# A down projection whose moving operand holds both halves of the weights

## The chip, the cores and the metric

The kernel runs on one core of one Trainium2 chip. The metric is the time on the device in microseconds. A profile comes from one more execution of the same program; its times are counted from its first instruction. Matmuls run on TensorE, and five instruction streams (TensorE, VectorE, ScalarE, GpSimd and SyncE) are written out by hand and joined by semaphores only.

## What is computed

A layer of gated cross attention and then a mixture of experts, over 16 x 256 = 4096 tokens of width 256, in float32. The change lies in the second half:

```python
logits = xf @ w_router
scores = softmax(logits); expert_weights, expert_indices = top_k(scores, 2)
h = silu(einsum('td,edh->teh', xf, w1)) * einsum('td,edh->teh', xf, w3)
y = einsum('teh,ehd->ted', h, w2)
moe_out = einsum('te,ted->td', cw, y)            # cw: the two chosen weights of a token
shared = silu(xf @ ws1) * (xf @ ws3) @ ws2
out = shared / 3 + moe_out * 2 / 3
x = x + tanh(g_ffn[0]) * out
```

There are 8 experts and one shared expert, each with 512 hidden units.

## The kernel before

**Numbers in two halves.** Each float32 operand of a projection is split into a high half (what the fast matmul format holds) and a low half (the rest), and a product is the sum of three: high x high, low x high, high x low. `three` (L580) issues these three matmuls for each chunk k of 128 contraction rows. The weights of an expert lie in `w_h[p]` and `w_l[p]`, three sets p: two change between the routed experts, the third (`SHARED`) holds the shared expert.

**Tiles.** After the attention stage (to about 345 us), 50 tiles of 256 tokens follow one another on TensorE: 6 early shared tiles, 34 routed tiles (tokens gathered by expert, four or five tiles an expert), 10 late shared tiles (batches 6 to 15). Each has 24 matmuls for `w1` (`up1`), 24 for `w3` (`up3`) and 24 for `w2` (`down`), all with 256 moving columns. TensorE's order for tile g (function `tile`) is `up1(g)`, `up3(g)`, `down(g-1)`. The last tile is taken apart and ends the kernel.

**Who does what in a tile g.** ScalarE: `silu(g)` of `up1`'s banks, the high half of the next tile's tokens (`xg_h`), a copy of the result of `down(g-1)` out of bank 5, the high half of the gated values (`gT_h`). VectorE: for routed tiles a transposition (`turn_rows`, L1490), the low half of the next tokens (`xg_l`), `gated(g)`, which multiplies `sg` with `up3`'s banks into `gg` (L1502), and `g_low(g)`, the low half `gT_l` (L1292). `up1(g)` waits for `xl_ok` (`xg_l`), `up3(g)` for `g_ok` of the tile before, and `down(g)` for `gl_ok` (`gT_l`) and `y_ok` (the result bank is free again).

**Results of routed tiles.** ScalarE's `y_before` (L1159) waits for the landing of the scatter before (`y_st`) and copies the bank to `y_s`; GpSimd's `scatter_y` (L1835) then sends its rows to `y_d` by row numbers that SyncE has fetched after the same landing. Between scatters GpSimd cuts the weights of the expert after next (`cut`, L1699 and L1703) in three parts, two before the first scatter of an expert and one behind it.

**Results of late shared tiles.** VectorE adds them from the bank into `x2a` (`add_late`, L1613), then mixes two finished batches with the routed results (`mix`, L1621 and L1626, each two operations, and a wait on its own result between) and, from batch 11 on, adds routed results of the last two batches (`add_pair`, L1636). SyncE stores each mixed batch; `mix` waits for the store of two batches before.

## Time and profile before

| | |
|---|---|
| Median of 3 runs | 798.59 us (797.7 to 800.58) |
| Profiled execution | 794.88 us, of which its span is 793.0 us |
| TensorE matmul | 765.8 us busy, 97% of the span |
| Weight loads (beside the matmuls) | 686.7 us, 87% |
| VectorE | 532.5 us, 67% |
| ScalarE | 423.5 us, 53% |
| GpSimd | 427.4 us, 54% |
| Granted TensorE clock, mean | 0.996 of full speed |

A busy share is a mean over stages. The stretches differ: attention until about 345 us, early shared tiles until about 420, routed tiles until about 710, late shared tiles until the end.

### The profile page before, as it was taken

What the parts mean: (1) busy time and instruction counts of PE and PEld (TensorE: products, weight loads), DVE (VectorE), ACT (ScalarE), POOL (GpSimd) and SP (SyncE); (2) the same over time, 40 slices, a digit from 0 to 9 for tenths busy, and PEclk for the clock granted to TensorE, in tenths of its full rate; (3) what the DMA queues carried; (4) which work ended last, traced back from release to release, by engine and by line L of the source; (5) the groups of instructions that cost most, each with busy time, mean ns of one, the idle gap of its engine ahead of it and who ended that gap; (6) DMA issues with size and microseconds to landing.
All of it is one profiled execution on the core that took longest, in us unless ns stands there. A gap on an engine that the chain in (4) does not pass through costs nothing.

```text
span 793.0 us, 19410 instructions
## 1 busy us (share of the span) xinstructions
PE 765.8 (97%) x6965; PEld 686.7 (87%) x6966; DVE 532.5 (67%) x1108; ACT 423.5 (53%) x717; POOL 427.4 (54%) x498
## 2 busy tenths in 40 slices
PE   5789999999999998999999999999999999999998
PEld 5666777777777776779999999999999999999998
DVE  6766788999888888856764544454344454456897
ACT  5767877777777777663344333333333333333332
POOL 5633447776666655376572659475846493235000
PEclk9989999999999999999999999999999999999999
DMA  6864557776666654253453646454533323218522
GB/s 210 270 201 162 177 189 238 241 241 217 212 217 215 212 179 143 95 201 134 133 153 97 171 140 186 116 141 114 159 89 106 97 53 80 54 60 340 217 84 81
DMA packets 130689, 127.36 MB, mean 161 GB/s; under 512 B 55232, under 2 KB 113088, under 8 KB 130624
## 3 DMA queue, kind: packets, MB, share of 16 engines
q1 hardware_dynamic: 117008, 82.44, 34.7%
q0 software_dynamic: 13616, 44.08, 15.8%
q8 instruction: 37, 0.61, 0.3%
q14 instruction: 28, 0.23, 0.1%
HBM read 75.32 MB, written 50.91 MB: 159 GB/s over the span
## 4 chain that ended last, share of the span: by engine, by line
PE 70%; POOL 8%; DMA 7%; DVE 5%; issue 5%; ACT 3%; POOLq 1%; SPq 0%; ACTq 0%; DVEq 0%
PE bank L586 8%; PE bank L587 7%; PE bank L588 7%; PE bank L676 7%; PE bank_ss L645 6%; PE bank_ss L586 4%; PE bank_ss L588 4%; PE bank_sm L586 4%; PE bank_ss L587 4%; POOL w_l L1703 4%; PE bank_sm L587 4%; PE bank_sm L588 4%; PE bank_sm L660 4%; DMA y_d<-y_s,y_rows 3%; PE bank L683 3%
## 5 line engine op out<-in xcount | busy, mean ns | idle before, releaser
L1315 DVE TENSOR_REDUCE row_max<-bank_sm 128x4 f32<-128x1024 f32 x124 | 151.6, 1222 | 40.8 <-PE bank_sm L660 40.3
L1000 ACT ACTIVATE probs_T<-bank_ss 128x1024 f32<-128x1024 f32 x123 | 126.5, 1028 | 19.1 <-PE bank_ss L645 18.9
L1292 DVE TENSOR_TENSOR gT_l<-gg,gT_h 128x1024 fp32r<-128x1024 f32 x49 | 69.3, 1415 | 100.2 <-ACT gT_h L1149 100.1
L586 PE MATMUL bank_sm<-xg_h,w_h 128*128 128x256 f32 x400 | 113.4, 283 | 0.5 <-DVE xg_l L1292 0.5
L586 PE MATMUL bank_ss<-xg_h,w_h 128*128 128x256 f32 x400 | 113.3, 283 | 0.4 <-DVE gg L1502 0.4
L587 PE MATMUL bank_sm<-xg_h,w_l 128*128 128x256 f32 x400 | 112.9, 282 | 0.0
L588 PE MATMUL bank_ss<-xg_l,w_h 128*128 128x256 f32 x400 | 112.9, 282 | 0.0
L588 PE MATMUL bank_sm<-xg_l,w_h 128*128 128x256 f32 x400 | 112.9, 282 | 0.0
L587 PE MATMUL bank_ss<-xg_h,w_l 128*128 128x256 f32 x400 | 112.9, 282 | 0.0
L586 PE MATMUL bank<-w_h,gT_h 128*128 128x256 f32 x392 | 111.1, 284 | 1.6 <-DVE gT_l L1292 1.6
L587 PE MATMUL bank<-w_h,gT_l 128*128 128x256 f32 x392 | 110.9, 283 | 0.0
L588 PE MATMUL bank<-w_l,gT_h 128*128 128x256 f32 x392 | 110.7, 282 | 0.0
L1753 POOL TENSOR_TENSOR qk_s<-qk_s 128x512 fp32r<-128x512 f32 x32 | 41.2, 1288 | 92.7 <-ACT qk_s L1052 92.6
L1835 POOL DMA_INDIRECT y_d<-y_s,y_rows x68 | 70.8, 1041 | 17.0 <-issue 15.8
L1143 ACT ACTIVATE sg<-bank_sm 128x512 f32<-128x512 f32 x98 | 53.2, 596 | 47.9 <-PE bank_sm L588 47.9
L1052 ACT ACTIVATE qk_s<-bank,bqk_s 128x256 f32<-128x256 f32 (+1 forms) x128 | 53.5, 480 | 47.1 <-PE bank L588 47.1
L586 PEld LDWEIGHTS bank_sm<-xg_h,w_h 128*128 128x128 f32 x400 | 76.4, 191 | 1.3 <-DVE xg_l L1292 0.7
L586 PEld LDWEIGHTS bank_ss<-xg_h,w_h 128*128 128x128 f32 x400 | 76.3, 191 | 0.7 <-DVE gg L1502 0.7
L586 PEld LDWEIGHTS bank<-w_h,gT_h 128*128 128x128 f32 x392 | 74.8, 191 | 2.2 <-DVE gT_l L1292 2.2
L587 PEld LDWEIGHTS bank_ss<-xg_h,w_l 128*128 128x128 f32 x400 | 76.4, 191 | 0.0
L587 PEld LDWEIGHTS bank_sm<-xg_h,w_l 128*128 128x128 f32 x400 | 76.4, 191 | 0.0
L588 PEld LDWEIGHTS bank_ss<-xg_l,w_h 128*128 128x128 f32 x400 | 76.4, 191 | 0.0
(210 smaller groups left out, 1956.0 us busy)
## 6 DMA issues: line engine op xcount, KB each, us to landing
qk_d<-qk_s SPq DMA_DIRECT2D x64, 256.0 KB, 2.7
w_raw<-wall POOLq DMA_DIRECT2D x27, 512.0 KB, 3.9
k<-qk_d SPq DMA_DIRECT2D x48, 256.0 KB, 3.9
q<-qk_d SPq DMA_DIRECT2D x48, 256.0 KB, 4.5
xq<-xs_d SPq DMA_DIRECT2D x140, 64.0 KB
y_pairs<-y_d POOLq DMA_DIRECT2D x16, 512.0 KB, 9.8
xs_d<-zero_rows SPq DMA_DIRECT2D x8, 514.0 KB, 4.6
x<-x SPq DMA_DIRECT2D x16, 256.0 KB, 4.3
```

Source lines behind the costliest of these rows:

```text
L586: pe.matmul(out, ah, bh, start=first and k == 0, stop=False)
L587: pe.matmul(out, al, bh, start=False, stop=False)
L588: r = pe.matmul(out, ah, bl, start=False, stop=last and k == n - 1)
L645: r = pe.matmul(exp_bank(V.b, pv)[:, par * 512 + half * L:par * 512 + (half + 1) * L], k4[V.slot][own, pv, half * P:(half + 1) * P], q4[V. ...
L676: r = pe.matmul(OT[g % 2][PVW * i:PVW * (i + 1), :], v_s[V.v_slot][:, kc, h, :], pT[:, h % 8, kc * L:(kc + 1) * L], start=kc == 0, stop=kc ...
L1000: act.activation(pT[:, 2 * (pv % 4):2 * (pv % 4) + 2, :].rearrange("p h t -> p (h t)"), exp_bank(V.b, pv)[:, :], ACT.Exp, scale=D ** -0.5) ...
L1052: r = act.activation(dst.bitcast(F32) if half else dst, bnk[:, oc * L:(oc + 1) * L], ACT.Identity, bias=bqk_s[:, 2 * side + oc:2 * side + ...
L1143: r = act.activation(sg[:, 2 * n:2 * n + 2, :].rearrange("p f t -> p (f t)"), psH1[n][:, :], ACT.Silu)
L1292: return v.tensor_tensor(dst, ps, high.bitcast(F32), ALU.subtract)
L1315: v.tensor_reduce(mx[B.slot][:, :, :].rearrange("p t (q r) -> p r t q", r=2)[:, :, :, p], max_bank(B.b, p)[:, :].rearrange("p (r t k) -> p ...
L1753: po.tensor_tensor(rest, rest.bitcast(F32), high.bitcast(F32), ALU.subtract).then_inc(done, 1)
L1835: po.indirect_dma_start(out=yd, out_offset=bass.IndirectOffsetOnAxis(ap=to[:, t:t + 1].bitcast(U32), axis=0), in_=y_s[:, t, :], in_offset= ...
```

## The change

The high and low halves of a set of weights become one tensor, `w_hl[p]`, so that one matmul can stream the high and the low half of the same 256 columns as one moving operand of 512. Result banks 5 and 6 become one tensor `Y2`. In the wide form of `down`, each chunk has one matmul of `gT_h` with both halves (512 columns) and one of `gT_l` with the high half (256 columns) instead of three of 256. The result of a tile then lies in two parts, `y_parts[0]` and `y_parts[1]`, whose sum is wanted. Wide are the projections of the 34 routed tiles and of the late shared tiles but the last; the six early ones stay as they were.

For routed tiles ScalarE copies the second part to `y_b` (`y_rest`), and VectorE adds it to the first part into `y_s` (`y_sum`, between `gated` and `g_low`), after waiting for the landing of the scatter before. For late shared tiles `add_late`, and the same step for batch 14, is two operations with a wait on the first's result between.

```diff
@@ -156,8 +156,8 @@
         wraw = sb(keep, "w_raw", [P, WSZ])
-        w_h0 = sb(keep, "w_h0", [P, WSZ], F32R)
-        w_l0 = sb(keep, "w_l0", [P, WSZ], F32R)
+        w0 = sb(keep, "w0", [P, 2, WSZ], F32R)
+        w_h0, w_l0 = w0[:, 0, :], w0[:, 1, :]
         tab = sb(keep, "table", [1, TW], I32)
...
@@ -233,17 +233,14 @@
             with ExitStack() as w:
-                w_h, w_l = [], []
-                for i in range(2):
-                    w_h.append(sb(w, f"w_h{i + 1}", [P, WSZ], F32R))
-                    w_l.append(sb(w, f"w_l{i + 1}", [P, WSZ], F32R))
-                w_h.append(w_h0)
-                w_l.append(w_l0)
+                w_hl = [sb(w, f"w_hl{i + 1}", [P, 2, WSZ], F32R) for i in range(2)] + [w0]
+                w_h, w_l = [u[:, 0, :] for u in w_hl], [u[:, 1, :] for u in w_hl]
             yg = sb(m, "y_pairs", [P, NB, TS, 2, E])
             x2a = sb(m, "x2_all", [P, NB, TS * E])
             xq = sb(m, "xq", [P, TR // QD, FQ])
             y_s = sb(m, "y_s", [P, TS, E])
+            y_b = sb(m, "y_rest", [P, TS, E])
             go = sb(m, "go", [P, 2])
...
@@ -264,7 +261,11 @@
         bank = [SS[:, 0:512], SS[:, 512:1024], SM[:, 0:512], SM[:, 512:1024]]
-        bank += [keep.enter_context(nc.psum_tensor(f"bank{i}", [P, 512], F32)) for i in range(4, 8)]
+        bank.append(keep.enter_context(nc.psum_tensor("bank4", [P, 512], F32))[:, :])
+        Y2 = keep.enter_context(nc.psum_tensor("bank56", [P, 1024], F32))
+        bank += [Y2[:, 0:512], Y2[:, 512:1024]]
+        bank.append(keep.enter_context(nc.psum_tensor("bank7", [P, 512], F32))[:, :])
+        y_parts = [Y2[:, :].rearrange("p (t s d) -> p t s d", t=TS, s=2)[:, :, n, :] for n in range(2)]
...
@@ -612,10 +613,24 @@
-            def down(g, p):
+            def down(g, p, wide=False):
                 pe.wait_ge(gl_ok, g + 1)
                 pe.wait_ge(y_ok, g + 1)
+                if wide:
+                    for t in range(TS):
+                        def high(k):
+                            return pe.matmul(Y2[:, t * 2 * E:(t + 1) * 2 * E].rearrange("p (s d) -> p s d", s=2), gT_h[:, k, t * P:(t + 1) * P],
+                                             w_hl[p][:, :, W2O + k * E:W2O + (k + 1) * E], start=k == 0, stop=k == FC - 1)
+
+                        for k in range(FC):
+                            if k < FC - 1:
+                                high(k)
+                            pe.matmul(Y2[:, t * 2 * E:t * 2 * E + E], gT_l[:, k, t * P:(t + 1) * P],
+                                      w_h[p][:, W2O + k * E:W2O + (k + 1) * E], start=False, stop=False, skip_group_check=True)
+                        r = high(FC - 1)
+                    r.then_inc(w2_ps, 1)
+                    return
                 for t in range(TS):
...
@@ -912,11 +927,11 @@
-            def tile(g, p, before):
+            def tile(g, p, before, wide=True):
                 up1(g, p)
                 up3(g, p)
-                down(g - 1, before)
+                down(g - 1, before, wide)
...
@@ -926,7 +941,7 @@
                 pe.wait_ge(w_ok, k * WP + 2 * WP)
-                tile(tb, p, before)
+                tile(tb, p, before, before != SHARED)
                 te = ends if isinstance(ends, list) else [value(T_E, k + i, EARLY + 2, EARLY + NT) for i in range(ends)]
...
@@ -955,7 +970,7 @@
                 r.then_inc(last_up, 1)
-            down(end + (NB - 2 - EARLY), SHARED)
+            down(end + (NB - 2 - EARLY), SHARED, True)
             for n in range(2):
...
@@ -1152,11 +1167,10 @@
-            def y_before(g, sent):
+            def y_rest(g):
                 act.wait_ge(w2_ps, g)
-                moved(act, y_st, sent * 32)
-                act.activation(y_s[:, :, :].rearrange("p t d -> p (t d)"), psY[:, :], ACT.Copy).then_inc(y_ok, 1)
+                act.activation(y_b[:, :, :], y_parts[1], ACT.Copy).then_inc(yb_ok, 1)
...
@@ -1203,22 +1217,22 @@
             x_high_routed(EARLY + 2)
-            y_before(EARLY + 1, 0)
+            y_rest(EARLY + 1)
             g_high(EARLY + 1)
             with act.Fori(1, last2) as u:
                 silu(u + (EARLY + 1))
                 x_high_routed(u + (EARLY + 2))
-                y_before(u + (EARLY + 1), u)
+                y_rest(u + (EARLY + 1))
                 g_high(u + (EARLY + 1))
             silu(last)
             x_high_shared(EARLY, end)
-            y_before(last, last2)
+            y_rest(last)
             g_high(last)
             for j in range(EARLY, NB - 1):
                 silu(end + (j - EARLY))
                 x_high_shared(j + 1, end + (j + 1 - EARLY))
                 if j == EARLY:
-                    y_before(end, last2 + 1)
+                    y_rest(end)
                 g_high(end + (j - EARLY))
...
@@ -1507,6 +1521,12 @@
+            def y_sum(copied, sent):
+
+                v.wait_ge(yb_ok, copied)
+                moved(v, y_st, sent)
+                v.tensor_tensor(y_s[:, :, :], y_parts[0], y_b[:, :, :], ALU.add).then_inc(y_ok, 1)
+
             iterations(v, one)
...
@@ -1597,11 +1617,18 @@
                 score_weights(b)
-            with v.Fori(EARLY + 1, last) as g:
-                turn_rows(g + 1)
-                x_low_routed(g + 1)
-                gated(g)
-                g_low(g)
+            last2 = v.value_load(tab[0:1, T_L2:T_L2 + 1], min_val=2 * NX - 2, max_val=NT - 2)
+            turn_rows(EARLY + 2)
+            x_low_routed(EARLY + 2)
+            gated(EARLY + 1)
+            y_sum(1, 0)
+            g_low(EARLY + 1)
+            with v.Fori(1, last2) as u:
+                turn_rows(u + (EARLY + 2))
+                x_low_routed(u + (EARLY + 2))
+                gated(u + (EARLY + 1))
+                y_sum(u + 1, u * 32)
+                g_low(u + (EARLY + 1))
...
@@ -1610,7 +1637,9 @@
                 v.wait_ge(w2_ps, end + (j + 1 - EARLY))
-                v.scalar_tensor_tensor(x2a[:, j, :], psY[:, :], gsc[:, 0:1], x2a[:, j, :], ALU.mult, ALU.add).then_inc(y_ok, 1)
+                x2j = x2a[:, j, :].rearrange("p (t d) -> p t d", t=TS)
+                link(v.scalar_tensor_tensor(x2j, y_parts[0], gsc[:, 0:1], x2j, ALU.mult, ALU.add))
+                v.scalar_tensor_tensor(x2j, y_parts[1], gsc[:, 0:1], x2j, ALU.mult, ALU.add).then_inc(y_ok, 1)
...
@@ -1649,6 +1679,8 @@
                         add_pair(*PAIR_AT[j])
+                    if j == EARLY:
+                        y_sum(last2 + 2, (last2 + 1) * 32)
                     g_low(end + (j - EARLY))
...
@@ -1673,7 +1705,9 @@
             v.wait_ge(o_st[b % 2], (b // 2) * 16)
-            v.scalar_tensor_tensor(o_o[b % 2][:, :, :].rearrange("p t d -> p (t d)"), psY[:, :], gsc[:, 0:1], x2a[:, b, :], ALU.mult, ALU.add).then_inc(mix_ok, 1)
+            x2b = x2a[:, b, :].rearrange("p (t d) -> p t d", t=TS)
+            link(v.scalar_tensor_tensor(x2b, y_parts[0], gsc[:, 0:1], x2b, ALU.mult, ALU.add))
+            v.scalar_tensor_tensor(o_o[b % 2][:, :, :], y_parts[1], gsc[:, 0:1], x2b, ALU.mult, ALU.add).then_inc(mix_ok, 1)
             b = NB - 1
```

TensorE, a down projection in the loop of late shared tiles, before (the names give result, stationary and moving operand, and the moving columns stand last):

```order
L586 MATMUL bank<-w_h,gT_h 128x256
L587 MATMUL bank<-w_h,gT_l 128x256
L588 MATMUL bank<-w_l,gT_h 128x256
L586 MATMUL bank<-w_h,gT_h 128x256
L587 MATMUL bank<-w_h,gT_l 128x256
L588 MATMUL bank<-w_l,gT_h 128x256
```

And the same place in the changed kernel:

```order
L623 MATMUL bank<-w,gT_h 128x512
L629 MATMUL bank<-w,gT_l 128x256
L623 MATMUL bank<-w,gT_h 128x512
L629 MATMUL bank<-w,gT_l 128x256
L623 MATMUL bank<-w,gT_h 128x512
L629 MATMUL bank<-w,gT_l 128x256 x2
L623 MATMUL bank<-w,gT_h 128x512 x2
```

Of 24 matmuls and weight loads a tile 16 are left, with the same 6144 columns; the last of four chunks has its short matmul first.

VectorE, the loop over routed tiles, before:

```order
L1490 STREAM_TRANSPOSE bank<-xq 128x512
L1494 REGISTER_ALU
L1292 TENSOR_TENSOR xg_l<-bank,xg_h 128x512
L1502 TENSOR_TENSOR gg<-sg,bank_ss 128x512 x2
L1292 TENSOR_TENSOR gT_l<-gg,gT_h 128x1024
```

And in the changed kernel:

```order
L1504 STREAM_TRANSPOSE bank<-xq 128x512
L1508 REGISTER_ALU
L1306 TENSOR_TENSOR xg_l<-bank,xg_h 128x512
L116 REGISTER_ALU
L1516 TENSOR_TENSOR gg<-sg,bank_ss 128x512 x2
L1526 REGISTER_ALU
L116 REGISTER_ALU
L1528 TENSOR_TENSOR y_s<-bank,y_rest 128x512
L1306 TENSOR_TENSOR gT_l<-gg,gT_h 128x1024
```

The add stands ahead of `gT_l`, for which TensorE's down projection waits.

VectorE, a late shared tile with mixes and a pair, before:

```order
L1292 TENSOR_TENSOR xg_l<-xsT,xg_h 128x512
L1502 TENSOR_TENSOR gg<-sg,bank_ss 128x512 x2
L1636 SCALAR_TENSOR_TENSOR x_all<-y_pairs,router_wts,x_all 128x256 x2
L1292 TENSOR_TENSOR gT_l<-gg,gT_h 128x1024
L1613 SCALAR_TENSOR_TENSOR x_all<-bank,gate_scaled,x_all 128x512
L1621 SCALAR_TENSOR_TENSOR y_pairs<-y_pairs,router_wts,x_all 128x256 x2
L1626 SCALAR_TENSOR_TENSOR oo<-y_pairs,router_wts 128x256 x2
```

And in the changed kernel:

```order
L1306 TENSOR_TENSOR xg_l<-xsT,xg_h 128x512
L1516 TENSOR_TENSOR gg<-sg,bank_ss 128x512 x2
L1665 SCALAR_TENSOR_TENSOR x_all<-y_pairs,router_wts,x_all 128x256 x2
L1306 TENSOR_TENSOR gT_l<-gg,gT_h 128x1024
L1641 SCALAR_TENSOR_TENSOR x_all<-bank,gate_scaled,x_all 128x512
L1642 SCALAR_TENSOR_TENSOR x_all<-bank,gate_scaled,x_all 128x512
L1650 SCALAR_TENSOR_TENSOR y_pairs<-y_pairs,router_wts,x_all 128x256 x2
L1655 SCALAR_TENSOR_TENSOR oo<-y_pairs,router_wts 128x256 x2
```

One operation more stands ahead of the mixes, and behind them the next tile's `xg_l`.

## Rows read from the trace of the kernel before

**Rows 1.** Table of stretches: start:end, length, busy us and (instructions) per engine, clock, DMA.

```profile
600.00:715.00 115.00, 115.00 (x962) 115.00 (x962) 53.79 (x70) 42.99 (x67) 59.97 (x63) 1.00 0.28 76
715.00:770.00 55.00, 55.00 (x464) 55.00 (x463) 43.30 (x79) 17.74 (x26) 11.70 (x17) 1.00 0.62 228
...
sum 793.00, PE 765.83 PEld 686.67 DVE 532.47 ACT 423.55 POOL 427.37; mean PE 127.64 PEld 114.45 DVE 88.75 ACT 70.59 POOL 71.23
```

**Rows 2.** Page, costliest groups: count, busy us, mean ns, idle before.

```profile
L586 PE MATMUL bank<-w_h,gT_h 128*128 128x256 f32 x392 | 111.1, 284 | 1.6 <-DVE gT_l L1292 1.6
```

**Rows 3.** Warm-up by line L628, ns min/median/max; timelines: start, us, then what.

```profile
L628 PEld LDWEIGHTS bank_ss<-wt_h x14: 187/188/189, 18.4 to 25.9; 128*128 128x128 f32 x14
L628 PE MATMUL bank_ss<-wt_h x14: 388/390/397, 18.5 to 26.2; 128*128 128x512 f32 x14
...
18.53 1.76 PE L628 MATMUL bank_ss<-wt_h 128*128 128x512 f32 x7
...
331.74 0.97 PEld L745 LDWEIGHTS bank<-wr_s,xn2T 128*128 128x128 f32 x8 [0.18 <-ACT xn2T L1013]
```

**Rows 4.** TensorE's waits, 440 to 600: us, times, longest; then the chain of waits.

```profile
PE bank L586 <- DVE gT_l L1292: 1.6, 3, 0.7
...
575.07 1.67 DVE gT_l L1292
576.78 0.39 PE bank L586
```

**Rows 5.** Timeline of ScalarE: y_s copies, in brackets idle before and its releaser.

```profile
439.46 0.60 ACT L1159 ACTIVATE y_s<-bank 128x512 f32<-128x512 f32 x1 [2.30 <-PE bank L588]
...
573.49 0.60 ACT L1159 ACTIVATE y_s<-bank 128x512 f32<-128x512 f32 x1 [5.13 <-DMA y_d<-y_s,y_rows]
...
616.49 0.60 ACT L1159 ACTIVATE y_s<-bank 128x512 f32<-128x512 f32 x1 [4.04 <-DMA y_d<-y_s,y_rows]
```

**Rows 6.** Timeline of GpSimd and of VectorE while expert weights are cut.

```profile
445.08 2.55 POOL L1703 TENSOR_TENSOR w_l<-w_raw,w_h 128x512 fp32r<-128x512 f32 x2
...
449.65 3.53 POOL L1703 TENSOR_TENSOR w_l<-w_raw,w_h 128x512 fp32r<-128x512 f32 x2
...
446.44 1.27 DVE L1502 TENSOR_TENSOR gg<-sg,bank_ss 128x512 f32<-128x512 f32 x2
449.68 2.35 DVE L1292 TENSOR_TENSOR gT_l<-gg,gT_h 128x1024 fp32r<-128x1024 f32 x1 [1.97 <-ACT gT_h L1149]
```

**Rows 7.** Timeline of VectorE, late shared tiles.

```profile
759.13 0.69 DVE L1292 TENSOR_TENSOR xg_l<-xsT,xg_h 128x512 fp32r<-128x512 f32 x1
759.74 1.28 DVE L1502 TENSOR_TENSOR gg<-sg,bank_ss 128x512 f32<-128x512 f32 x2
...
762.14 1.23 DVE L1292 TENSOR_TENSOR gT_l<-gg,gT_h 128x1024 fp32r<-128x1024 f32 x1 [0.34 <-ACT gT_h L1149]
763.29 0.74 DVE L1613 SCALAR_TENSOR_TENSOR x_all<-bank,gate_scaled,x_all 128x512 f32<-128x512 f32 x1
763.95 0.87 DVE L1621 SCALAR_TENSOR_TENSOR y_pairs<-y_pairs,router_wts,x_all 128x256 f32<-128x256 f32 x2
764.86 0.88 DVE L1626 SCALAR_TENSOR_TENSOR oo<-y_pairs,router_wts 128x256 f32<-128x256 f32 x2
...
767.37 0.69 DVE L1292 TENSOR_TENSOR xg_l<-xsT,xg_h 128x512 fp32r<-128x512 f32 x1
...
770.68 1.23 DVE L1292 TENSOR_TENSOR gT_l<-gg,gT_h 128x1024 fp32r<-128x1024 f32 x1 [0.62 <-ACT gT_h L1149]
```

**Rows 8.** Timeline of VectorE, late shared tiles of batches 8 and 9.

```profile
724.50 0.69 DVE L1292 TENSOR_TENSOR xg_l<-xsT,xg_h 128x512 fp32r<-128x512 f32 x1 [3.38 <-ACT xg_h L1132]
...
741.65 0.88 DVE L1626 SCALAR_TENSOR_TENSOR oo<-y_pairs,router_wts 128x256 f32<-128x256 f32 x2 [0.73 <-DMA out<-oo]
```

**Rows 9.** Timeline of VectorE, the end.

```profile
788.44 0.74 DVE L1676 SCALAR_TENSOR_TENSOR oo<-bank,gate_scaled,x_all 128x512 f32<-128x512 f32 x1
789.67 0.48 DVE L1681 SCALAR_TENSOR_TENSOR oo<-bank,gate_scaled,x_all 128x256 f32<-128x256 f32 x1 [0.48 <-PE bank L588]
```

More of the change, by code:

```diff
@@ L304, in build @@
         gh_ok = sem("gh_ok"); gl_ok = sem("gl_ok"); w2_ps = sem("w2_ps"); last_up = sem("last_up"); last_sg = sem("last_sg"); last_g = sem("last_g"); last_gh = sem("last_gh"); last_gl = sem("last_gl"); last_w2 = sem("last_w2"); last_mix = sem("last_mix"); last_st = sem("last_st")
-        y_ok = sem("y_ok"); y_st = sem("y_st"); to_in = sem("to_in"); go_ok = sem("go_ok"); tok_ok = sem("tok_ok"); x2_in = sem("x2_in")
+        y_ok = sem("y_ok"); yb_ok = sem("yb_ok"); y_st = sem("y_st"); to_in = sem("to_in"); go_ok = sem("go_ok"); tok_ok = sem("tok_ok"); x2_in = sem("x2_in")
         yg_in = [sem(f"yg_in{i}") for i in range(NB)]
@@ L1641, in _ @@
             gated(last)
+            y_sum(last2 + 1, last2 * 32)
             g_low(last)
```

## The prediction

> **What bounds the kernel now.** I read the table of stretches first, then TensorE's own waits, then the chain of waits backwards from each of them. TensorE is busy for 765.8 of 793 us, and without a gap from 600 to 770, while VectorE has work for 43.3 of the 55 us from 715 to 770 [rows 1]. So a step that TensorE loses there is gained, as long as nobody else is nearly late. Two parties are nearly late, and the busy shares hide both.
>
> The first is GpSimd from 440 to 600. TensorE's only waits in the routed tiles are three for `gT_l`, the longest 0.7 us by that view, one each in three of the experts [rows 4]. The chain leads back from the one at 576.78 over `gT_l` [rows 4] and `gT_h` to the `y_s` copy at 573.49, which a scatter's landing released, and from there for 130 us over GpSimd and its transfers alone (cutting weights, scatter, landing, row numbers, scatter) to the copy at 439.46 [rows 5]. In that stretch GpSimd sets the pace by a hair.
>
> The second is VectorE in the late shared tiles. One tile there runs from 759.13 to 767.37, 8.24 us, and in it VectorE waits for nothing but 0.34 us for `gT_h`, which itself follows VectorE's own `gg` [rows 7]. TensorE needs 55.00/464 x 72 = 8.53 us a tile [rows 1]. This is a serial chain with a slack of 0.3 us a tile, not an engine with a fifth of its time free.
>
> **What the change removes.** A tile has 72 matmuls of 256 columns, 24 of them down, at 115.00/962 = 0.120 us each [rows 1]; a triple takes 0.36. The wide form issues one of 512 and one of 256. The only 512-column stream is the warm-up at 18.53: seven in 1.76 us, the last lasting 0.39, so (1.76 - 0.39)/6 = 0.229 us each [rows 3]. A triple becomes 0.229 + 0.120 = 0.349: 0.011 saved, 8 triples a tile, 0.09 us. There are 392 such triples in 49 down projections [rows 2], the last tile's aside; six early shared ones stay narrow, 43 go wide: 3.8 us in all. The ends: nothing (the two-piece moving operand costs what the load saved), and 0.035 a triple (0.28 a tile) if the loads are what sets 0.12 now; loads alone come every (0.97 - 0.19)/7 = 0.111 us [rows 3]. I take 0.011, since its row has both a full load and 512 columns in each step.
>
> The Trainium skill, "TensorE: Matmul & The Clock Gate", section "Back-to-back issue gap", gives 262 cycles for 256 columns and 518 for 512, so that merging two saves 6 cycles, 2.5 ns: 0.9 us over 344 triples where the rows say 3.8. The spacing of 120 ns here is 11 above that page's 109, so I hold to the rows.
>
> **What of that arrives, routed tiles.** ScalarE's copy goes to `y_b` and no longer waits for the scatter; VectorE does the waiting and adds, 0.64 us (as half of the `gg` pair, also one PSUM and one SBUF operand [rows 7]), between `gated` and `g_low`. Behind it on VectorE stand `g_low`, for which TensorE's next down projection waits, and the row turn.
> Where TensorE sets the pace the add runs beside ScalarE's `gT_h` of 1.05 and costs nothing. But `y_ok` comes 0.7 us later and GpSimd's scatter with it. So GpSimd's chain starts at 439.46 with three wide projections gained (-0.27) and 0.7 lost: 0.45 us later. At 573.49 its landing is thus at 573.94. From there before: copy, `gT_h`, `gT_l` (1.67), start at 576.78, 3.29 us [rows 4, 5]. After: add 0.6, `gT_l` 1.67, semaphores 0.05 to 0.1, 2.35 to 2.8, since `gT_h` is already done; I take 2.77, since the add may be stretched beside GpSimd's `w_l` as `gT_l` is in [rows 6]. The projection starts at 576.7 - 0.5 = 576.26: only **0.5 us** of the 1.5 us saved up to there is kept, and TensorE waits some 1.0 us more than before in sum. Five tiles later, at the landing of 616.49 [rows 5], the two are level again: 0.9. From there 11 routed projections bring 11 x 0.09 = 1.0. At 715 us TensorE is **2.0 us early** (ends: 0 and 5, the latter with 0.28 a tile over 16 tiles and 0.5 before).
>
> **What of that arrives, late shared tiles.** `add_late` becomes two operations with a wait on its own result between. One takes 0.74, 0.66 to the next start; where VectorE waits on its own result now, the next starts 0.04 after the end instead of 0.08 before [rows 7]. So each adds 0.74 + 0.04 = 0.78 us to VectorE. The first of the eight falls into 3.38 us of idle [rows 8]. The other seven stand in tiles with two mixes: 7 x 0.78 = 5.5 us on a chain with no idle. It absorbs the two waits for stored outputs (0.73 [rows 8] and one of 0.2) and the excess of the last two `gT_h` waits over 0.34 (0.62 [rows 7], so 0.3 each): 1.5 us. The end of the kernel hangs on this chain: the final up projections wait for `gated` of batch 14, and VectorE's last multiplications for the mixes before them. Behind them the doubled add at 788.44 ends at 789.9 rather than 789.2 and moves the next one, at 789.67 [rows 9], by 0.2, of which the last keeps 0.1. Sum: 5.5 - 1.5 + 0.1 = **4.1 us later**; TensorE's 9 wide projections here bring 0.2 (three before VectorE takes over), the rest is lost in new waits of about 0.5 us before each `up1`.
>
> **Sum.** 794.88 - 2.0 - 0.2 + 4.1 = 796.8 us for the profiled execution, +1.9. The median is 798.59 of runs from 797.7 to 800.58, above the profiled one by 3.7; I carry the difference over: **800.5 us**.
>
> **The rivals.**
> *GpSimd is slowed (slower).* `w_l` takes 2.55 us for two passes, but 3.53 where `gT_l` falls on it [rows 6]: 0.98 for one collision. If the new add, or a `gT_l` shifted onto a pass, costs that once in each expert from the third on, the landing at 576 comes 3 us later, at 616 4 us; TensorE enters the late tiles 2.1 us behind instead of 2.0 ahead, and the late loss stays: +6, 804.6. It decides from some 0.5 us per expert on. For it: there is no slack in GpSimd's chain. Against: the add has one operand in PSUM, like `gg`, and `gg` at 446.44 ran beside the 2.55 row [rows 6] without stretching it.
> *The late additions hide (faster, within 0.5%).* VectorE is idle for 11.7 us from 715 to 770, and 8 x 0.78 is 6.2 [rows 1]. Then 2.0 + 0.7 come through: 795.9. Against it is the serial order in [rows 7].
> *Loads set the spacing.* 0.28 a tile: 5.0 early at 715, then VectorE's chain paces the rest and takes 3.6 back: 797.2. The same page's section "LDWEIGHTS" has columns / 1.2, 107 ns for 128; by it the wide pair would cost 216 + 109 ns, this rival. The warm-up [rows 3] has 0.229 where that load is hidden, against it.
> *The wide form saves nothing.* 0.5 early at 715, 4.1 late: 802.2.
>
> **How the numbers follow.** A change of 0.5%, 4 us, is about what a measurement here can tell from none. Forecast 0.55; loads 0.12; hidden 0.10; no saving 0.08; GpSimd slowed 0.12; something else 0.03. Of the forecast's and the no-saving case's own spread (1.5 us in the sum, 1 us in a median of three) some 0.1 lies beyond 802.6. So faster 0.07, same 0.74, slower 0.19. The range takes in loads and hidden and half of the GpSimd case: 795.8 to 804.0.
>
> **What would show it.** Spacing in the profile after: 0.23 behind each 512-column matmul, 0.12 behind the 256 (0.35 a pair); 0.325 speaks for loads. A down projection of 2.79 instead of 2.88. Waits for `gT_l` near 497, 541 and 577, of 1 us or more. In the late tiles VectorE's pitch 9.0, with TensorE waiting some 0.5 before each `up1` from batch 11 on, and about 1.8 before the last. `w_l` passes no longer than before. I am wrong if the late pitch stays at 8.5 (hidden), or if TensorE is late already at 715 us (GpSimd).

## The result, and the profile after

The changed kernel takes 800.01 us (median of 20 runs, 795.82 to 803.58), the kernel before 797.26 us (20 runs, 794.65 to 802.27). The medians differ by 2.8 us. The ratio, which isn't quite the quotient of the medians, is 1.0036 with a 95% interval of 1.0020 to 1.0051 (1.6 to 4.1 us longer): a small loss, within the 0.5% that I called no change. The forecast was 800.5 us.

The profiled execution has a span of 797.0 us where the kernel before had 793.0. I split it at two points that both traces show: A, the first matmul of `up1` of the second routed tile (the last before any wide projection), and B, the first matmul of `up1` of batch 8, the third late tile. Between them lie 34 routed down projections and one late one. I call the last part, from B on, the end stage.

| | start to A | A to B | B to end | span |
|---|---|---|---|---|
| before | 413.27 | 304.61 | 75.12 | 793.0 |
| after | 415.20 | 301.56 | 80.24 | 797.0 |
| difference | +1.93 | -3.05 | +5.12 | +4.0 |

The first difference is not the change's: nothing in that part is computed otherwise, and over all profiles of this study A lies anywhere from 412.88 to 416.81, the earliest in a kernel with wide projections, the latest in one with narrow ones.

First the page's lines of busy time and of the costliest groups that answer to [rows 2], and the table of stretches that answers to [rows 1] (start:end, length, busy us and instructions of TensorE, its weight loads, VectorE, ScalarE and GpSimd, then clock and DMA).

```profile
PE 764.6 (96%) x6621; PEld 668.3 (84%) x6622; DVE 556.9 (70%) x1151; ACT 426.2 (53%) x717; POOL 430.3 (54%) x498
...
L623 PE MATMUL bank<-w_hl,gT_h 128*128 128x512 f32 x272 | 96.0, 396 | 1.6 <-DVE gT_l L1306 1.5
```

```profile
600.00:715.00 115.00, 115.00 (x865) 110.30 (x864) 63.40 (x84) 43.78 (x68) 63.54 (x63) 1.00 0.28 76
715.00:770.00 55.00, 53.13 (x394) 49.95 (x393) 44.84 (x80) 16.68 (x24) 11.79 (x17) 1.00 0.60 218
770.00:797.00 27.00, 21.54 (x156) 19.53 (x154) 22.14 (x41) 6.20 (x9) 0.00 (x0) 1.00 0.24 80
```

TensorE is still full from 600 to 715, and no longer from 715 on: it is without work for 1.9 of the 55 us there, and for 5.5 in the last stretch, what follows its last matmul among them. TensorE's own timeline shows both, a routed projection without a wait and two late tiles that begin with one.

```profile
448.39 0.39 PE L623 MATMUL bank<-w_hl,gT_h 128*128 128x512 f32 x1
448.62 0.28 PE L629 MATMUL bank<-w_hl,gT_l 128*128 128x256 f32 x1
448.74 0.40 PE L623 MATMUL bank<-w_hl,gT_h 128*128 128x512 f32 x1
...
752.11 0.40 PE L623 MATMUL bank<-w,gT_h 128*128 128x512 f32 x1
752.81 0.39 PE L587 MATMUL bank_sm<-xg_h,w 128*128 128x256 f32 x1 [0.30 <-DVE xg_l L1306]
...
781.14 0.36 PE L587 MATMUL bank_sm<-xg_h,w 128*128 128x256 f32 x1 [1.48 <-DVE gg L1516]
```

A pair takes 448.74 - 448.39 = 0.35 us, of which 0.23 behind the 512 columns. At 752.81 the next matmul would have been due at 752.11 + 0.23 = 752.34, so 0.47 are lost.

TensorE's waits, first from 440 to 600 [rows 4], then from 715 to the end (in all, times, longest):

```profile
PE bank L623 <- DVE gT_l L1306: 1.5, 1, 1.5
...
PE bank_sm L587 <- DVE xg_l L1306: 2.1, 4, 1.3
PE bank_sm L587 <- DVE gg L1516: 1.5, 1, 1.5
```

VectorE's timeline in the late tiles, which answers to [rows 7] and [rows 8] (in brackets idle before, and its releaser):

```profile
741.40 0.88 DVE L1655 SCALAR_TENSOR_TENSOR oo<-y_pairs,router_wts 128x256 f32<-128x256 f32 x2 [0.60 <-DMA out<-oo]
743.05 0.69 DVE L1306 TENSOR_TENSOR xg_l<-xsT,xg_h 128x512 fp32r<-128x512 f32 x1 [0.76 <-ACT xg_h L1147]
...
752.07 0.69 DVE L1306 TENSOR_TENSOR xg_l<-xsT,xg_h 128x512 fp32r<-128x512 f32 x1
...
755.08 1.22 DVE L1306 TENSOR_TENSOR gT_l<-gg,gT_h 128x1024 fp32r<-128x1024 f32 x1 [0.34 <-ACT gT_h L1164]
756.23 0.74 DVE L1641 SCALAR_TENSOR_TENSOR x_all<-bank,gate_scaled,x_all 128x512 f32<-128x512 f32 x1
757.00 0.75 DVE L1642 SCALAR_TENSOR_TENSOR x_all<-bank,gate_scaled,x_all 128x512 f32<-128x512 f32 x1
757.67 0.87 DVE L1650 SCALAR_TENSOR_TENSOR y_pairs<-y_pairs,router_wts,x_all 128x256 f32<-128x256 f32 x2
...
761.09 0.68 DVE L1306 TENSOR_TENSOR xg_l<-xsT,xg_h 128x512 fp32r<-128x512 f32 x1
```

From one `xg_l` to the next, the pitch of VectorE's chain, it is 761.09 - 752.07 = 9.02 us, where it was 8.24 [rows 7]. The second addition is the whole difference: it starts 0.77 behind the first, and the only idle time in the tile is the same 0.34 for `gT_h`. The end, which answers to [rows 9]:

```profile
792.10 0.74 DVE L1709 SCALAR_TENSOR_TENSOR x_all<-bank,gate_scaled,x_all 128x512 f32<-128x512 f32 x1
792.88 0.75 DVE L1710 SCALAR_TENSOR_TENSOR oo<-bank,gate_scaled,x_all 128x512 f32<-128x512 f32 x1
793.55 0.48 DVE L1715 SCALAR_TENSOR_TENSOR oo<-bank,gate_scaled,x_all 128x256 f32<-128x256 f32 x1
```

### The profile page after: what moved, and what is told of

The parts are those of the page before. It is cut to its first block, busy times and chain, and to the rows that moved or that the text cites. A ratio compares the mean times of both kernels' runs of the same rounds, so it can differ in the third digit from the quotient of the medians.

```text
span 797.0 us, 18828 instructions
## 1 busy us (share of the span) xinstructions
PE 764.6 (96%) x6621; PEld 668.3 (84%) x6622; DVE 556.9 (70%) x1151; ACT 426.2 (53%) x717; POOL 430.3 (54%) x498
## 4 chain that ended last, share of the span: by engine, by line
PE 63%; DVE 10%; POOL 8%; DMA 8%; issue 6%; ACT 3%; POOLq 1%; SPq 0%; DVEq 0%; ACTq 0%
PE bank L691 7%; PE bank_ss L660 6%; PE bank L587 5%; PE bank L623 5%; POOL w_hl L1737 4%; PE bank L588 4%; PE bank L589 4%; PE bank_sm L675 4%; PE bank_ss L587 3%; PE bank_ss L589 3%; PE bank_ss L588 3%; PE bank_sm L587 3%; PE bank_sm L588 3%; PE bank_sm L589 3%; DMA y_d<-y_s,y_rows 3%
## 5 line engine op out<-in xcount | busy, mean ns | idle before, releaser
L623 PE MATMUL bank<-w_hl,gT_h 128*128 128x512 f32 x272 | 96.0, 396 | 1.6 <-DVE gT_l L1306 1.5
L589 PE MATMUL bank_ss<-xg_l,w_hl 128*128 128x256 f32 x272 | 77.1, 284 | 0.0
L588 PE MATMUL bank_sm<-xg_h,w_hl 128*128 128x256 f32 x272 | 77.1, 283 | 0.0
L587 PE MATMUL bank_ss<-xg_h,w_hl 128*128 128x256 f32 x272 | 77.1, 283 | 0.0
L589 PE MATMUL bank_sm<-xg_l,w_hl 128*128 128x256 f32 x272 | 77.0, 283 | 0.0
L588 PE MATMUL bank_ss<-xg_h,w_hl 128*128 128x256 f32 x272 | 76.9, 283 | 0.0
L587 PE MATMUL bank_sm<-xg_h,w_hl 128*128 128x256 f32 x272 | 76.8, 282 | 0.0
L1737 POOL TENSOR_TENSOR w_hl<-w_raw,w_hl 128x512 fp32r<-128x512 f32 x48 | 71.8, 1515 | 2.0
L1776 POOL DMA_INDIRECT xs_d<-xn,slot_i x64 | 64.2, 1003 | 15.6 <-issue 14.3
L691 PE MATMUL bank<-probs_T,v 128*32 128x256 f32 x1024 | 69.4, 389 | 0.0
L660 PE MATMUL bank_ss<-q,k 64*128 64x256 f32 x492 | 63.0, 333 | 5.8 <-ACT probs_T L1015 5.4
L1516 DVE TENSOR_TENSOR gg<-sg,bank_ss 128x512 f32<-128x512 f32 x98 | 62.5, 680 | 5.8 <-PE bank_ss L589 5.8
```

Source lines behind the costliest of these rows:

```text
L587: pe.matmul(out, ah, bh, start=first and k == 0, stop=False)
L588: pe.matmul(out, al, bh, start=False, stop=False)
L589: r = pe.matmul(out, ah, bl, start=False, stop=last and k == n - 1)
L623: return pe.matmul(Y2[:, t * 2 * E:(t + 1) * 2 * E].rearrange("p (s d) -> p s d", s=2), gT_h[:, k, t * P:(t + 1) * P], w_hl[p][:, :, W2O + ...
L660: r = pe.matmul(exp_bank(V.b, pv)[:, par * 512 + half * L:par * 512 + (half + 1) * L], k4[V.slot][own, pv, half * P:(half + 1) * P], q4[V. ...
L691: r = pe.matmul(OT[g % 2][PVW * i:PVW * (i + 1), :], v_s[V.v_slot][:, kc, h, :], pT[:, h % 8, kc * L:(kc + 1) * L], start=kc == 0, stop=kc ...
```

## The experiments

All medians, intervals and parts in one table; each kernel ran beside the kernel before on the same chip. Differences in microseconds below are worked out from the ratio, which differs from the quotient of the two medians by up to about 0.1% (for "routed wide only" the medians are 2.6 us apart and the ratio gives 2.0). A to B and B to end are read from the one profiled execution, and so are TensorE's waits in the routed tiles (waits of 0.15 us and more); one execution differs there from the next, so a difference of a microsecond between two rows can be chance.

| kernel | median | before beside it | ratio [95%] | A to B | routed waits | B to end |
|---|---|---|---|---|---|---|
| before | | | | 304.61 | 1.6 | 75.12 |
| after | 800.01 | 797.26 | 1.0036 [1.0020, 1.0051] | 301.56 | 1.5 | 80.24 |
| routed wide only | 793.27 | 795.87 | 0.9975 [0.9954, 0.9995] | 301.87 | 1.5 | 76.14 |
| late wide only | 799.83 | 795.87 | 1.0051 [1.0034, 1.0068] | 304.58 | 1.7 | 78.89 |
| added operation only | 799.98 | 795.87 | 1.0050 [1.0033, 1.0068] | 305.10 | 2.2 | 78.87 |
| result path only | 795.24 | 795.87 | 0.9996 [0.9979, 1.0013] | 302.97 | 0.2 | 76.34 |
| GpSimd adds | 800.78 | 796.78 | 1.0055 [1.0038, 1.0071] | 303.42 | 3.0 | 81.71 |
| GpSimd adds, load first | 800.88 | 796.78 | 1.0049 [1.0031, 1.0068] | 304.94 | 3.6 | 81.38 |
| after, load first | 799.39 | 796.78 | 1.0032 [1.0017, 1.0046] | 304.06 | 3.5 | 79.42 |
| routed wide, load first | 794.01 | 796.78 | 0.9963 [0.9945, 0.9980] | 303.35 | 2.9 | 75.15 |
| the same, sum behind `gT_l` | 792.77 | 797.66 | 0.9933 [0.9908, 0.9957] | 299.90 | 0.2 | 75.54 |
| before, load first | 798.89 | 797.66 | 1.0004 [0.9979, 1.0029] | 306.01 | 2.8 | 75.18 |

### The two halves of the change apart

Routed tiles wide, the late ones and batch 14 as before with one addition (the main lines):

```diff
-                tile(g, SHARED, SHARED)
+                tile(g, SHARED, SHARED, False)
...
-                link(v.scalar_tensor_tensor(x2j, y_parts[0], gsc[:, 0:1], x2j, ALU.mult, ALU.add))
-                v.scalar_tensor_tensor(x2j, y_parts[1], gsc[:, 0:1], x2j, ALU.mult, ALU.add).then_inc(y_ok, 1)
+                v.scalar_tensor_tensor(x2a[:, j, :], psY[:, :], gsc[:, 0:1], x2a[:, j, :], ALU.mult, ALU.add).then_inc(y_ok, 1)
```

> Wide down projections for the 34 routed tiles only; the late shared tiles are narrow again with one add each. Theory (two separate terms, a gain in the routed tiles and a loss on VectorE's late chain): about 3 us faster than the kernel before (2 by the prediction's sum, 3.05 by the trace of the changed kernel), ratio 0.996 to 0.9975, down projection 2.80 us, late VectorE pitch 8.2 to 8.5 as before. Rival (the 1.9 us by which the changed kernel's trace is late already at 400 us comes from the merged weight tensors): it stays here, so only 1 us faster and the first wide projection again 1.9 us late. Rival (GpSimd's chain takes the routed gain): no change.

Late tiles wide, the routed ones as before (ScalarE's `y_before` straight to `y_s`; the main lines):

```diff
-                    tile(g, p, p)
+                    tile(g, p, p, False)
...
-                act.activation(y_b[:, :, :], y_parts[1], ACT.Copy).then_inc(yb_ok, 1)
+                moved(act, y_st, sent * 32)
+                act.activation(y_s[:, :, :].rearrange("p t d -> p (t d)"), psY[:, :], ACT.Copy).then_inc(y_ok, 1)
```

> Routed tiles narrow with ScalarE's copy as in the kernel before; only the late shared tiles are wide with the doubled add. Theory (VectorE's serial chain is the bound there): 4 to 5 us slower, ratio 1.005 to 1.0065, VectorE's pitch 9.0 us from batch 10 on, TensorE waits 0.3 to 0.7 before each of its first up projections from batch 11 and 1.5 to 1.9 before the last tile. Rival (the additions hide in VectorE's idle time): 0.7 us faster, no such waits.

The first is 2.0 us faster than before (0.4 to 3.7), the second 4.1 slower (2.7 to 5.4). Their sum, +2.1, agrees with the +2.8 of the whole within the intervals. So the change is a gain and a loss that nearly cancel, each in its own stage.

### The added operation by itself

The kernel before, with its narrow projections, and a second addition of zero times the bank behind the first, with the same wait between. Batch 14, not shown, has it too:

```diff
-                v.scalar_tensor_tensor(x2a[:, j, :], psY[:, :], gsc[:, 0:1], x2a[:, j, :], ALU.mult, ALU.add).then_inc(y_ok, 1)
+                link(v.scalar_tensor_tensor(x2a[:, j, :], psY[:, :], gsc[:, 0:1], x2a[:, j, :], ALU.mult, ALU.add))
+                v.scalar_tensor_tensor(x2a[:, j, :], psY[:, :], zero[:, 0:1], x2a[:, j, :], ALU.mult, ALU.add).then_inc(y_ok, 1)
```

> The kernel before, all projections narrow, with a second, linked add (times zero, from the same bank) behind each late add and behind that of batch 14: the added VectorE work alone, no wide matmul, no second bank. Theory: 4.1 us slower or up to 5, ratio 1.005 to 1.0065, pitch 9.0. Rival (the wide matmuls or the two-bank operand cost the time in the late tiles, not the operation): under 1 us slower.

It costs 4.0 us (2.6 to 5.4), as much as the wide late projections with their two additions. The end stage is 78.87 us long against 78.89 with the wide form: in the late tiles the wide form of TensorE brings and costs nothing that shows, and VectorE's operation is the whole loss. VectorE's timeline of this kernel has the pitch again, 771.20 - 762.19 = 9.01 us:

```profile
762.19 0.68 DVE L1292 TENSOR_TENSOR xg_l<-xsT,xg_h 128x512 fp32r<-128x512 f32 x1
...
766.34 0.74 DVE L1613 SCALAR_TENSOR_TENSOR x_all<-bank,gate_scaled,x_all 128x512 f32<-128x512 f32 x1
767.12 0.75 DVE L1614 SCALAR_TENSOR_TENSOR x_all<-bank,zero_rows,x_all 128x512 f32<-128x512 f32 x1
...
771.20 0.68 DVE L1292 TENSOR_TENSOR xg_l<-xsT,xg_h 128x512 fp32r<-128x512 f32 x1
```

### The path of the routed results by itself

The changed kernel with every projection narrow; the routed results still go over `y_b` on ScalarE and an operation on VectorE. The maximum of the bank and its own copy stands for the sum, so that the operation keeps its operands and nothing is left out:

```diff
-                v.tensor_tensor(y_s[:, :, :], y_parts[0], y_b[:, :, :], ALU.add).then_inc(y_ok, 1)
+                v.tensor_tensor(y_s[:, :, :].rearrange("p t d -> p (t d)"), psY[:, :], y_b[:, :, :].rearrange("p t d -> p (t d)"), ALU.max).then_inc(y_ok, 1)
```

> All projections narrow; only the way of the routed results is the changed one: ScalarE copies to y_b, VectorE waits for the scatter and forms y_s (here the larger of two equal values). Theory (the path is nearly neutral: y_ok 0.7 us later, 0.5 us back at the waits): within 1 us of before, w_l passes as long as before, waits for gT_l 0.5 us shorter each. Rival (GpSimd slowed): 2 us slower or more, with more passes of 3.5 us. If the path by itself gains, the routed gain of 3 us is partly not the matmuls': then 1 us faster.

The time does not move (-0.3 us, -1.7 to +1.0), but the trace does: TensorE waits 0.2 us for `gT_l` where it waited 1.6, and A to B is 1.6 us shorter than in the kernel before. That fits the prediction's view that it pays when `gT_h` no longer stands behind the landing. But it is one execution, and in the six kernels below that use this path with wide projections the waits are 1.5 to 3.6 us; how much of the routed gain is the path's and how much the matmuls' is not shown. The end stage gives 1.2 back: TensorE waits 1.1 us for tokens there, which leads to the next edit.

### The added operation on GpSimd

GpSimd is idle in the late tiles, so there the second part might cost nothing: ScalarE scales it into `y_b`, and GpSimd adds it. TensorE's next projection then waits for ScalarE's copy as well, and the projection of batch 14 is narrow again (both not shown).

```diff
+                    act.activation(y_b[:, :, :], y_parts[1], ACT.Identity, bias=zero[:, 0:1], scale=gsc[:, 0:1]).then_inc(yb_ok, 1)
...
-                link(v.scalar_tensor_tensor(x2j, y_parts[0], gsc[:, 0:1], x2j, ALU.mult, ALU.add))
-                v.scalar_tensor_tensor(x2j, y_parts[1], gsc[:, 0:1], x2j, ALU.mult, ALU.add).then_inc(y_ok, 1)
+                v.scalar_tensor_tensor(x2j, y_parts[0], gsc[:, 0:1], x2j, ALU.mult, ALU.add).then_inc(y_ok, 1)
...
+                po.tensor_tensor(x2j, x2j, y_b[:, :, :], ALU.add).then_inc(x2b_ok, 1)
```

> The changed kernel, except that in the late shared tiles VectorE keeps one addition: ScalarE copies the second result part, scaled by the gate, to y_rest, and GpSimd, which is idle there, adds it to the output sum; the last tile but one has the narrow projection. Theory (VectorE's serial chain paces the late tiles, and the added operation of 0.78 us is the whole loss): the late stage falls back from 80.2 us (first late tile to the end, changed kernel) to about 76 to 76.5, as where the late projections are narrow; time against the kernel before -1.5 to -2.5 us. Rival A (the wide form itself, or ScalarE's copy of 0.6 us behind the projection, holds the tiles): the late stage stays above 79, time +2 to +4. Rival B (GpSimd's additions of some 1.3 us slow VectorE where both run): pitch of the tiles with two mixes between 8.6 and 9.0 us, time 0 to +2.

My theory missed by some 6 us here: 4.4 us slower than before (3.0 to 5.7), an end stage of 81.71 us. VectorE's chain still sets the pace, and the time of the operation did not leave it. GpSimd's and VectorE's timelines:

```profile
757.97 1.40 POOL L1906 TENSOR_TENSOR x_all<-x_all,y_rest 128x512 f32<-128x512 f32 x1 [7.87 <-DVE x_all L1651]
```

```profile
757.08 0.74 DVE L1651 SCALAR_TENSOR_TENSOR x_all<-bank,gate_scaled,x_all 128x512 f32<-128x512 f32 x1
757.74 1.91 DVE L1660 SCALAR_TENSOR_TENSOR y_pairs<-y_pairs,router_wts,x_all 128x256 f32<-128x256 f32 x2
759.68 0.88 DVE L1665 SCALAR_TENSOR_TENSOR oo<-y_pairs,router_wts 128x256 f32<-128x256 f32 x2
760.48 0.88 DVE L1660 SCALAR_TENSOR_TENSOR y_pairs<-y_pairs,router_wts,x_all 128x256 f32<-128x256 f32 x2
```

While GpSimd adds from 757.97 to 759.37, VectorE's pair of mixes takes 1.91 us instead of the 0.88 of the same pair at 760.48: 1.03 us lost in place of the 0.77 that were taken away. All six such pairs from 738 us on take 1.91, each beside a GpSimd addition. The pitch is 9.27 us, which is 8.24 + 1.03. Rival B had the mechanism and too small a price.

### The load of the tokens

In the changed kernel TensorE waits 1.33 us before batch 11. VectorE's `xg_l` at 743.05 waited for ScalarE, and ScalarE for a load, by its timeline and SyncE's:

```profile
742.39 0.63 ACT L1147 ACTIVATE xg_h<-xsT 128x512 fp32r<-128x512 f32 x1 [4.47 <-DMA xsT<-xT_d]
```

```profile
731.03 2.10 SPq L563 DMA_DIRECT2D out<-oo  x2
733.29 0.38 SPq L465 DMA_DIRECT2D xsT<-xT_d  x1
```

SyncE issues it behind the two stores, and it lands 9.1 us later. Meanwhile the 16 `y_pairs` loads of GpSimd's queue are on the DMA engines: issued from 716.0 to 726.9, they take 4.9 to 15.3 us from issue to landing, and the last is in at 742.1. The next load of tokens, issued at 742.85, takes 2.7. The edit issues each such load one tile earlier, ahead of the stores (the one for batch 8, the loop's first instruction until now, stands ahead of the loop):

```diff
+            load_shared(EARLY + 2, total + (EARLY + 1))
             for j in range(EARLY + 2, NB):
-                load_shared(j, total + (j - 1))
+                if j + 1 < NB:
+                    load_shared(j + 1, total + j)
```

It was put on four kernels. On that with routed tiles wide and late ones narrow:

> Routed tiles wide, late tiles narrow with one addition on VectorE, and SyncE's load of a late batch's tokens ahead of the stores. Theory (as for the previous kernel): routed tiles wide alone gave -2.0 us (793.27 against 795.87) with TensorE waiting 0.7 us for tokens near 743 us; without that wait -2.7 to -3.3 us, the late stage 75.3 us instead of 76.1. Rival (the wait only moves): -2.0 us as before, the late stage 76.

On the changed kernel:

> The changed kernel with the load of a late batch's tokens ahead of the stores, and nothing else. Theory A (the late tiles are one serial chain on VectorE from batch 9 on, and a wait for tokens stretches it): -1.0 to -1.5 us against the changed kernel, so +1.3 to +1.8 against the kernel before; the late stage 79 us. Theory B (the chain on VectorE is late at 743 us by its own work, the tokens are not what it waits for): +2.8 as the changed kernel, the late stage 80.

On the one with GpSimd's addition:

> The previous kernel with one more edit: SyncE issues the load of a late batch's tokens ahead of the stores of the two mixed batches, one tile earlier. Theory (the tokens of batch 11, landing at about 742.3 us whether TensorE is early or not, give back about 1 us of what the routed tiles won): the wait of TensorE for xg_l near 743 us (1.5 us in the changed kernel) goes, and the time is 0.7 to 1.5 us below that of the previous kernel. Rival (VectorE's chain or its wait for the store of two batches before is late there anyway, or the load is as late behind the y_pairs loads): the wait moves to another name and the time is the same within 0.3 us.

And on the kernel before:

> The kernel before, with SyncE's load of a late batch's tokens ahead of the stores of the mixed batches. Theory (the load's landing at about 742 us is a limit only for a TensorE that comes early, since the kernel before has no wait of TensorE there): within 0.5 us of the kernel before, the late stage 75 us as there. Rival (the order of loads and stores is worth about 1 us by itself): -1 us.

With the routed tiles wide it is 2.9 us faster than the kernel before (1.6 to 4.4), TensorE's wait for tokens is gone and the end stage is 75.15 us instead of 76.14, as the theory had it. The kernel before gains nothing (+0.3 us, -1.7 to +2.3; end stage 75.18): the landing limits only a TensorE that comes early. On the changed kernel the wait falls from 1.3 to 0.4 us and the end stage by 0.8, between the two theories; its time, 1.0032, can't be told from 1.0036. With GpSimd's addition the wait falls from 1.5 to 1.2 only and the time is the same, which is the rival. The times of the two kernels with routed tiles wide, 0.9963 and 0.9975, can't be told apart either, so the 1.0 us rests on the profiles.

### The sum behind `gT_l`

The waits in the routed tiles remain, 1.5 to 3.6 us in the six kernels that are wide there. In VectorE's timeline of the changed kernel one looks like this:

```profile
497.54 0.69 DVE L1528 TENSOR_TENSOR y_s<-bank,y_rest 128x512 f32<-128x512 f32 x1 [5.32 <-DMA y_d<-y_s,y_rows]
498.15 1.46 DVE L1306 TENSOR_TENSOR gT_l<-gg,gT_h 128x1024 fp32r<-128x1024 f32 x1
```

The low half stands behind the landing and the addition. The last edit to the best kernel so far turns them round in the routed tiles:

```diff
-                y_sum(u + 1, u * 32)
                 g_low(u + (EARLY + 1))
+                y_sum(u + 1, u * 32)
```

> Routed tiles wide, late tiles narrow, token loads ahead of the stores, as in the kernel that gave 794.0 us against 796.8; and in the routed tiles VectorE's addition into y_s stands behind gT_l instead of ahead of it. Where the scatter's landing is late (498 and 577 us, TensorE idle 1.5 and 1.4 us), TensorE then waits for 0.7 us behind the landing instead of 2.1. Theory A (what counts is the place of gT_l behind the wait): both waits go, 1.4 to 2.9 us faster than that kernel, about -4.5 against the kernel before. Theory B (GpSimd's chain is full from about 440 us on, so the landing is as late as the first addition of the chain starts later, about 1.3 us): the waits stay within 0.5 us of what they were, under the name of the addition's semaphore, and the time is the same within 0.5 us: about -2.8 against the kernel before.

Theory A held, and theory B fell: 5.3 us faster than the kernel before (3.4 to 7.3), the best of all. TensorE has one wait of 0.2 us left in the routed tiles. B was right that the first addition, and with it GpSimd's chain, starts later, but wrong that the chain has no slack. GpSimd's timeline, first with the sum ahead of `gT_l`, then behind:

```profile
440.99 0.19 POOL L1865 TENSOR_TENSOR go<-go 128x1 f32<-128x1 f32 x1 [4.80 <-DVE y_s L1530]
441.33 1.82 POOL L1867 DMA_INDIRECT y_d<-y_s,y_rows  x1 [0.15 <-issue]
...
450.95 3.41 POOL L1735 TENSOR_TENSOR w_hl<-w_raw,w_hl 128x512 fp32r<-128x512 f32 x2
...
463.54 0.22 POOL L1865 TENSOR_TENSOR go<-go 128x1 f32<-128x1 f32 x1
```

```profile
443.74 0.19 POOL L1865 TENSOR_TENSOR go<-go 128x1 f32<-128x1 f32 x1 [5.95 <-DVE y_s L1530]
444.08 0.99 POOL L1867 DMA_INDIRECT y_d<-y_s,y_rows  x1
...
452.93 2.55 POOL L1735 TENSOR_TENSOR w_hl<-w_raw,w_hl 128x512 fp32r<-128x512 f32 x2
...
464.53 0.22 POOL L1865 TENSOR_TENSOR go<-go 128x1 f32<-128x1 f32 x1
```

It starts 2.75 us later, of which 0.76 lie before A (414.36 here, 413.60 there), and is 0.99 later two scatters on: the first scatter's issue no longer runs beside `gT_l` (0.99 instead of 1.82), and one pass of the cut does not either (2.55 instead of 3.41). The addition that waits for the late landing starts at 496.70, against 496.17 with the sum ahead: 0.53 later from the start of the kernel, and 0.23 earlier counted from A. The two kernels ran on different chips, each beside the kernel before; by their ratios they are 2.4 us apart, which is hardly clear of the two intervals, so the step from the one to the other rests on the waits of the profiles, 2.9 us against 0.2.

## Why the prediction held, point by point

**The spacing.** 0.23 behind a 512-column matmul, 0.12 behind one of 256, 0.35 a pair: as forecast. A routed projection without a wait takes 2.80 to 2.81 us from its first matmul to the next `up1`, 0.07 to 0.08 less than 2.88; 34 of them bring 2.6 where I had 3.1, so the 0.011 us saved a merge was nearer 0.0095. The rival that loads set the spacing would have shown 0.325, and the one that the wide form saves nothing 0.36; both are out. By an estimate from the cycles that "TensorE: Matmul & The Clock Gate" of the Trainium skill gives in its section "Back-to-back issue gap", a merge saves 2.5 ns, 0.02 us a projection; the trace has 0.07 to 0.08.

**What arrives of it, routed tiles.** I had 2.0 us early at 715, because TensorE would wait 1.0 us more than before in sum. The profile of after has 3.05 and as little waiting as before (1.5 us), which looks like a miss. It is one draw: over the six kernels wide there with the sum ahead of `gT_l`, A to B is 303.2 on average and the waits 2.7 us; over the four with the old path (before, late wide only, added operation only, before with the load first) 305.1 and 2.1. That is 1.9 us early and 0.6 more waiting, so the term stands. Its size rests on few executions, which spread from 301.6 to 304.9 and from 304.6 to 306.0. The waits lie where I put them, near 498, 541 and 577, but not all in each execution. The step inside it was mis-sized, and the sum slipped: from the landing to the projection I had 2.77 us in place of 3.29, and added it to the old landing of 573.49 rather than to the later one of 573.94 that I had just worked out. With that, 576.71, only 0.07 us would have been kept, not 0.5. In the kernel with routed tiles wide and the load first, where that wait occurs, the addition starts at 575.12 and the projection at 577.24, 2.1 us, since `gT_l` took 1.46 rather than 1.67. Counted from A, that projection comes at 163.4 us on average over the six and at 164.1 over the four: 0.7 kept. So the 0.5 came out nearly right because two errors cancelled.

**The GpSimd rival** had more in it than I gave it. I said that its passes would be no longer than before. From 440 to 715, by the groups of before and of after:

```profile
L1703 POOL TENSOR_TENSOR w_l<-w_raw,w_h 128x512 fp32r<-128x512 f32 x36 | 50.5, 1421 | 1.5
```

```profile
L1869 POOL DMA_INDIRECT y_d<-y_s,y_rows x64 | 69.2, 1081 | 17.9 <-issue 17.6
L1737 POOL TENSOR_TENSOR w_hl<-w_raw,w_hl 128x512 fp32r<-128x512 f32 x36 | 54.4, 1531 | 1.5
```

Of 18 pairs of passes 5 were stretched to some 3.5 us before, and 9 are now. Four collisions more are 3.9 us of GpSimd's time. They come with the path of the results and not with the wide matmuls: with the path alone 8 are stretched, with only the late tiles wide 4. So my sign for this rival, longer passes, did appear. But the landing near 575 came 160.22 us behind A before (573.49 - 413.27) and 159.73 in the changed kernel; over the six kernels it is 161.3 on average (159.7 to 162.9) and over the four 160.7 (160.2 to 161.7). That is some 0.5 us later, as forecast (0.45), and not the rival's 3, though one of the six, GpSimd adds with the load first, comes near it. Where the chain makes the rest good was not taken apart; that it can is what the last experiment shows too.

**Late tiles.** The additions cost 0.77 each, the pitch is 9.02 (forecast 9.0), TensorE loses 0.47 before an `up1` (forecast 0.5) and idles 1.48 before the last one (1.8). The rival that they hide is out: the added operation alone costs 4.0 us. The mis-sized term is what the chain absorbs. I had 5.5 - 1.5 + 0.1 - 0.2 = 3.9, with VectorE's waits for stored outputs, 0.73 and 0.2, gone. Where TensorE is as late as before (late wide only, batch 8 at 719.61), they are gone indeed, and the end stage grows by 3.8. In the changed kernel it grows by 5.1, and the 1.3 more are the two waits of VectorE at 741.40 and 743.05, 0.60 us for a store and 0.76 for the tokens of batch 11. Without them that `xg_l` would start at 743.05 - 1.36 = 741.69, where with only the late tiles wide it starts at 744.49: VectorE comes 2.8 us earlier, but the load only 1.0 (it lands at 742.39 rather than 743.42). I had let the gain of the routed tiles pass, and not asked what it would meet. The edit to the load gives 0.8 of the 1.3 back.

**The sum.** +1.9 forecast; the profile has +4.0, of which 1.9 lie before A, so +2.1; the medians have +2.8 (1.6 to 4.1). That the forecast of 800.5 lies within 0.5 of the measured 800.01 is partly luck: it started from 798.59, the median of three runs, where twenty give 797.26, and this 1.3 too much made up for an increase forecast 0.9 too small. The mechanism held: a gain in the routed tiles against a loss on VectorE's serial chain in the late ones. What was mis-sized is how much of the seven additions that chain absorbs once TensorE comes early.

## What to carry to other kernels

Before a step is made cheaper by giving another engine one more operation, look at that engine's serial order in the stage, not at its busy share: at 79% busy (43.3 of 55 us) VectorE had 0.3 us of room a tile, and an operation of 0.77 cost all of itself. Keep such a form only in the stages where the helper has room; and put an operation that waits for a transfer behind the one for which TensorE waits, even when this starts the transfers later. Time won early in a kernel is kept only as far as the next load lets it through: see when that one is issued.

## What the hardware showed that I had not expected

**GpSimd and VectorE hold each other up, both ways, by most of an operation.** For the cut and `gT_l` it stands in [rows 6]: `w_l` 3.53 instead of 2.55 us where `gT_l` falls on it, and `gT_l` 2.35 in place of 1.23. New are VectorE's mixes, 1.91 instead of 0.88 us beside a GpSimd addition of 1.40, and the issue of a scatter, 1.82 instead of 0.99 beside `gT_l`. The issue is held up only where `gT_l` is already running when it begins: in the changed kernel `gT_l` started 0.26 us ahead of seven issues, and each took 1.82; in the kernel before seven issues began ahead of `gT_l`, and each took 0.99. In all of these VectorE reads two operands in SBUF. Its additions with one operand in the bank are never stretched, though nine of the 34 ran beside a pass of the cut, by the lines of the changed kernel's `y_s` and `gT_l` (ns min/median/max, first and last start):

```profile
L1528 DVE TENSOR_TENSOR y_s<-bank,y_rest x34: 691/692/693, 424.6 to 709.2; 128x512 f32<-128x512 f32 x34
```

```profile
L1306 DVE TENSOR_TENSOR gT_l<-gg,gT_h x49: 1206/1226/2326, 363.5 to 782.1; 128x1024 fp32r<-128x1024 f32 x49
```

This is what "SBUF — State Buffer" of the Trainium skill states in its section "Who interferes with whom": a VectorE instruction with two SBUF inputs contends with a GpSimd instruction that reads SBUF, and one with at most one SBUF input does not. The trace agrees with it, by the durations above. That page also infers that a `tensor_tensor` leaves the making of DMA descriptors on GpSimd alone; the scatter's issue, 0.83 us longer, speaks against that for indirect transfers.

**A moving operand in two pieces costs nothing that shows.** The high and the low half lie apart in `w_hl`, and 512 columns of them take 0.23 us, as the warm-up's contiguous ones do [rows 3].
